# Layers 1 and 2 experts: two buffers for copied down weights, each copied in its slot's own step; 22 unread products instead of 40 ahead of layer 1's first rows

## What is computed

```python
def _L1_ffn_ref(x, Wr, W1, W2, W3):          # 8 experts, hidden width 352
    logits = tokens @ Wr
    probs = softmax(logits); topw, tope = top_k(probs, 2)
    gate = sum(one_hot(tope, E) * topw[..., None], axis=1)
    a = einsum('td,edh->teh', tokens, W2)
    b = einsum('td,edh->teh', tokens, W1)
    y = einsum('teh,ehd->ted', silu(a) * b, W3)
    out = einsum('ted,te->td', y, gate)
```

## Time and profile before

| | us |
|---|---|
| median of 3 runs | 817.55 |
| lowest and highest | 816.50 and 820.42 |
| the profiled execution, its own time | 818.61 |
| its span, first to last instruction | 816.8 |
| PE busy | 715.4 (88%) |
| DVE busy | 437.7 (54%) |
| POOL busy | 308.8 (38%) |
| ACT busy | 244.9 (30%) |
| mean granted TensorE clock, share of full speed | 0.937 |

### The profile page before, as it was taken

How to read it: one execution, slowest core, us unless ns; L and a number is a source line. 1 busy time by engine, 2 the same in 40 slices (tenths; PEclk the granted TensorE clock), 3 DMA queues, 4 the chain that set the end, 5 groups by cost and what they waited for, 6 DMA issues and landing times. The chain is left out here.

```text
span 816.8 us, 16930 instructions
## 1 busy us (share of the span) xinstructions
PE 715.4 (88%) x6115; PEld 577.2 (71%) x6115; DVE 437.7 (54%) x1155; ACT 244.9 (30%) x624; POOL 308.8 (38%) x365
## 2 busy tenths in 40 slices
PE   7997798899999889989896898798998878979997
PEld 5785687788888768844475686675433745879997
DVE  3766967545434365656534655675684367532212
ACT  1132411355445043124502411243364035111120
POOL 2346441456664140234214224411453187253211
PEclk9997997899999999899998799798998979899999
DMA  9403004788886439645324802100463244256603
GB/s 361 193 14 48 5 1 143 246 243 240 240 236 192 139 81 413 243 143 186 113 74 106 317 2 46 19 2 33 121 199 102 67 71 199 81 199 234 236 17 106
DMA packets 76553, 116.60 MB, mean 143 GB/s; under 512 B 44023, under 2 KB 57528, under 8 KB 73528
## 3 DMA queue, kind: packets, MB, share of 16 engines
q1 hardware_dynamic: 65141, 90.95, 35.3%
q0 software_dynamic: 6912, 17.31, 6.7%
q10 hardware_dynamic: 4418, 7.26, 2.4%
HBM read 100.34 MB, written 15.16 MB: 141 GB/s over the span
## 5 line engine op out<-in xcount | busy, mean ns | idle before, releaser
L280 PE MATMUL ps<-const_sb 128*128 128x128 f32 x946 | 126.4, 294 | 5.7 <-DMA const_sb<-in_consts 4.8
L280 PEld LDWEIGHTS ps<-const_sb 128*128 128x128 f32 x946 | 121.2, 208 | 9.0 <-DMA const_sb<-in_consts 4.8
L1878 PE MATMUL ps<-l0e_xg_fm,l0e_ring 128*128 128x128 f32 x544 | 72.7, 277 | 6.3 <-ACT l0e_up_sb L1968 2.5
L1878 PEld LDWEIGHTS ps<-l0e_xg_fm,l0e_ring 128*128 128x128 f32 x544 | 67.6, 191 | 12.2 <-issue 7.7
L955 PE MATMUL ps<-x_fm,w_sb 128*128 128x296 f32 x208 | 54.5, 414 | 4.6 <-PEq L237 4.3
L2473 PE MATMUL ps<-l_w,const_sb 128*32 x132 | 48.8, 506 | 7.7 <-DMA l1e_own_gu<-in_l_experts 3.0
L308 POOL TENSOR_TENSOR norm_r<-norm_ve,const_sb 128x2 f32<-128x2 f32 (+1 forms) x27 | 19.5, 724 | 92.5 <-DVE norm_ve L301 68.2
L955 PEld LDWEIGHTS ps<-x_fm,w_sb 128*128 128x128 f32 x208 | 39.1, 190 | 17.5 <-issue 6.1
L1784 POOL DMA_INDIRECT l0e_y_scratch<-l0e_y_tm,l0e_rows_u x34 | 35.6, 1047 | 32.3 <-ACT l0e_y_tm L1992 28.2
L413 ACT ACTIVATE x_fm<-ps 128x256 f32<-128x256 f32 x35 | 12.5, 383 | 107.5 <-PE ps L389 107.4
L1769 POOL DMA_INDIRECT l0e_xg_tm<-x_scratch,l0e_rows_u x34 | 33.3, 979 | 23.5 <-PE ps L1842 10.1
(11 more groups left out here) (518 smaller groups left out, 1635.0 us busy)
## 6 DMA issues: line engine op xcount, KB each, us to landing
l0e_ring<-in_l_experts SPq DMA_DIRECT2D x34, 514.0 KB
l_w<-in_l_experts SPq DMA_DIRECT2D x1, 8704.0 KB, 27.4
expert_w<-in_l_experts SPq DMA_DIRECT2D x4, 2048.0 KB
l_more_w<-in_l_experts SPq DMA_DIRECT2D x4, 2048.0 KB
l1e_own_gu<-in_l_experts SPq DMA_DIRECT2D x11, 704.0 KB
l_w<-in_l_experts SPq DMA_DIRECT2D x1, 6144.0 KB, 18.8
l2e_own_gu<-in_l_experts SPq DMA_DIRECT2D x11, 512.0 KB
l0e_down_w<-in_l_experts SPq DMA_DIRECT2D x1, 4096.0 KB
```

Of the source, the lines that this page charges most:

```text
L280: pe.matmul(ps[:, bank, 0:P], ident, ident, start=True, stop=True)
L1878: mm = pe.matmul(ps[0:widths[m], which, m * P:(m + 1) * P], w_n[:, c:c + widths[m]], x_n[:, k, :], start=(k == 0), stop=(k == KT - 1))
```

## The change

- `own_dn` gets two buffers; slot n uses n % 2.
- ACT and DVE copy the down weights of slot r in step r, where they copied those of slot r-1. The wait in front is the same one: in step r the down products of slot r-2 must be done, since that slot had the same buffer. For slots 0 and 1 there is no wait. DVE's loop has 11 steps instead of 12, and ACT's copies end a step earlier.
- In layer 1, 22 unread products stand ahead of `turn(0)` instead of 40.
- `ROWS` becomes an argument, whose default of 4 is what both calls use, so nothing follows from it.

```diff
-                own_dn = sb(f"{tag}_own_dn", [P, G - 1, MT * D], where=st)
+                own_dn = sb(f"{tag}_own_dn", [P, G - 1, 2, MT * D], where=st)
...
-                            stay_awake(pe, 40)
+                            stay_awake(pe, 22)
                             turn(0)
...
-                                                       own_dn[:, c - 1, m * D:(m + 1) * D] if c
+                                                       own_dn[:, c - 1, (e - S) % 2, m * D:(m + 1) * D] if c
...
-                            if 1 <= r <= NS:
-                                if r == 1:
+                            if 0 <= r < NS:
+                                if r == 0:
                                     act.wait_ge(s_expert, 1)
                                     act.wait_ge(s_all, all_ready)
                                 if r >= 2:
                                     act.wait_ge(s_down, S + r - 1)
                                 for c in mine["act"][1]:
-                                    theirs = held_by(act, r - 1, c)
-                                    act.activation(own_dn[:, c - 1, :], whole(theirs, GU, GU + MT * D), ACT.Copy)\
+                                    theirs = held_by(act, r, c)
+                                    act.activation(own_dn[:, c - 1, r % 2, :], whole(theirs, GU, GU + MT * D), ACT.Copy)\
                                         .then_inc(s_dn[c], 1)
...
-                                if n >= 1:
-                                    dve.wait_ge(s_down, S + n)
+                                if n >= 2:
+                                    dve.wait_ge(s_down, S + n - 1)
...
-                        for n in range(NS + 1):
-                            if n < NS:
-                                hidden(S + n)
-                                if n + 2 < NS:
-                                    copy_gu(n + 2)
-                            if n >= 1:
-                                copy_dn(n - 1)
+                        for n in range(NS):
+                            hidden(S + n)
+                            if n + 2 < NS:
+                                copy_gu(n + 2)
+                            copy_dn(n)
```

More of the change, by code:

```diff
@@ L2238, in column_experts @@
         def column_experts(tag, held, w_in, E, top, H, R, gu_by, dn_by, after, ahead=(), bias=None, dense=None, source=None,
-                           diag_in=None):
+                           diag_in=None, ROWS=4):
             G = P // R
@@ L2246, in column_experts @@
             NT = NS * G
-            ROWS, YS = 4, 3
+            YS = 3
             S, first = (0, 0) if dense is None else (TILES, 1)
@@ L2291, in column_experts @@
                 own_gu = sb(f"{tag}_own_gu", [P, G - 1, 2, GU], where=st)
-                own_dn = sb(f"{tag}_own_dn", [P, G - 1, MT * D], where=st)
-                xg_tm = row_sb[:, YS * D:(YS + ROWS) * D].rearrange("p (u d) -> p u d", d=D)
+                own_dn = sb(f"{tag}_own_dn", [P, G - 1, 2, MT * D], where=st)
+                xg_tm = row_sb[:, YS * D:(YS + ROWS) * D].rearrange("p (u d) -> p u d", d=D) if ROWS == 4 \
+                    else sb(f"{tag}_xg_tm", [P, ROWS, D], where=st)
                 xg_fm = const("pe")[:, 0:2 * KT * P].rearrange("p (u k r) -> p u k r", u=2, k=KT)
@@ L2713, in copy_dn @@
                             for c in mine["dve"][1]:
-                                if n >= 1:
-                                    dve.wait_ge(s_down, S + n)
+                                if n >= 2:
+                                    dve.wait_ge(s_down, S + n - 1)
                                 whose = experts[n, c] if (n, c) in experts else held_by(dve, n, c)
-                                dve.tensor_copy(own_dn[:, c - 1, :], whole(whose, GU, GU + MT * D)).then_inc(s_dn[c], 1)
+                                dve.tensor_copy(own_dn[:, c - 1, n % 2, :], whole(whose, GU, GU + MT * D))\
+                                    .then_inc(s_dn[c], 1)
                         dve.wait_ge(s_expert, 1)
```

## The result

| | before | changed |
|---|---|---|
| median, us | 817.02 (4 runs) | 805.07 (4 runs) |
| lowest to highest | 815.9 to 820.42 | 802.24 to 809.99 |
| the profiled execution's own time | 818.61 | 809.99 |
| its span | 816.8 | 808.2 |

The ratio is 0.9856, with a 95% interval of 0.9819 to 0.9893. Two later comparisons of the same two kernels gave 0.9872 (0.9822 to 0.9921) and 0.9887 (0.9853 to 0.9921). Ratios and intervals here leave out runs more than 1.5% above the fastest run of their kernel; the medians and ranges keep them. So the change saves 1.1 to 1.4% of the time, 9 to 12 us. The profiled execution happens to be the slowest of the four. Total times of this kernel scatter: on one chip 29 runs of the kernel before ranged from 806.6 to 823.1 us.

What follows compares the result with a forecast made beforehand. PE was taken as working nearly without a gap, idling for own_dn only at the loops' ends. Gains of 4.13 (front), 4.27 and 4.34 us (ends) sum to 12.7, off 818.61 gives 805.9 us; 8-in-10 range 802.5 to 810.0.

Steps and rivals of the forecast that it cites:

- The ends of the loops: Last two slots of each layer's loop: waits for own_dn and low clock vanish, 4.27 us in layer 1, 4.34 in layer 2.
- The landing: Behind each loop, the outputs' way back rather than unread products becomes the limit: 0.32 us saved in layer 1, 0.86 in layer 2.
- rival 1: Clock falls anyway at both ends, or mostly didn't fall before; only idle times go, 10.3 us, 808.3 us; chance 0.22.
- The front: Ahead of layer 1's slots: 18 unread products fewer at 0.2295 us each, gain 4.13 us.
- has landed at about 346.5, 0.8 us ahead of need: Layer 1's front: the first gather's rows are there before `turn(0)` at 347.32, so it needn't wait.
- A wait of `turn(0)` for the gather: Layer 1's front: listed first among signs of being wrong; `turn(0)` should follow the unread products without a wait.
- My bound of 3.3 us for the front: Layer 1's front: lowest gain allowed, for gather 0 landing 0.8 us late; upper bound 4.13.
- the second assumption: Layer 1's front: the unread products run at full clock, 0.2295 us each, 22 in 5.05 us.
- Rival 2: Layer 1's front: first rows late, two slots wait, 0.4 to 1.5 us lost, 807 us; chance 0.15 together with Rival 3.
- Rival 3: Loop ends: slot 10's hidden values late behind ACT's copy, 1.5 us lost, 807.4 us; chance 0.15 together with Rival 2.
- Rival 4: Layer 1's slots: fewer unread products drop the clock to 1.2 GHz, 809.4 us for one stretch, up to 833; chance 0.04.
- Rival 5: Loop ends: slot 10's copies still come last, so only the front's gain stays, 814.5 us; chance 0.02.

Runs made afterwards that it cites:

- Experiment 11: Changed kernel with 20 instead of 28 unread products behind the loops of layers 1 and 2: 807.89 us, ratio 0.9945 against the kernel before.
- experiment 2: Kernel before with only the front shortened, 22 instead of 40 unread products ahead of layer 1's slots, one buffer: 809.25 us, ratio 0.9965 against the kernel before.
- experiment 3: The changed kernel itself, run again on the first chip: 800.96 us, ratio 0.9872 against the kernel before.
- experiment 9: The changed kernel itself, run once more on the third chip: 804.68 us against 814.86 for the kernel before, ratio 0.9887.
- experiment 6: Changed kernel with 14 instead of 22 unread products ahead of layer 1's slots, second chip: 786.30 us, ratio 0.9843 against the kernel before.
- experiment 5: Changed kernel with none of the 22 unread products ahead of layer 1's slots: 791.06 us against 800.87 for the kernel before, ratio 0.9863.
- Experiment 7: Changed kernel, but in layer 1 ACT instead of DVE copies own_gu for slots 0 and 1: 787.68 us, ratio 0.9853 against the kernel before.
- experiment 4: Kernel before with unread products put into its four waits for own_dn: 811.37 us, ratio 0.9989 against the kernel before.
- experiment 1: Changed kernel with 40 unread products in front as before, so only the two buffers: 805.49 us against 814.17 for the kernel before, ratio 0.9916.
- experiment 8: Changed kernel with ACT making layer 1's own_gu copies for slots 0 and 1, and 14 unread products in front: 790.01 us, ratio 0.9882 against the kernel before.
- experiment 10: Changed kernel with 14 unread products ahead of layer 1's slots, third chip: 806.49 us, ratio 0.9902 against the kernel before.

## Why the prediction was right, and where a step was not

The time was right: 805.9 forecast, 805.07 measured, inside the range of 802.5 to 810.0, and faster as forecast. That the two differ by only 0.8 us is luck, since the forecast took 12.7 us off and the change is worth some 9 to 12.

**The ends of the loops** came out step by step. In layer 1 slot 9's down products followed the transposes without a wait, slot 10's waited 0.17 us for the hidden values (about 0.1 predicted), and the stretch shrank by 4.03 us (3.95). In layer 2 the wait was 0.48 us and the stretch shrank by 3.46 (3.48). Reading the page's 1.33 us "for line 2579" as a wait for `own_dn` was right: it is gone. The landing became what is late, as said, 0.22 us better than forecast in layer 1 and 0.31 worse in layer 2; PE idled 0.40 and 1.16 us for it, where I had said 0.6 to 0.9. Experiment 11 showed that it is the limit. The four waits of before, and the low clock that came with them, were the whole of the buffers' gain; the steady steps had none to give. (In the bounds of layer 2's end, 3.02 - 0.33 is 2.69 and not 2.6; rival 1 has it as 2.7, and nothing else uses it.)

**The front** was mis-sized. The term "18 x 0.2295 = 4.13 us" gave 2.80, 2.40, 2.39, 3.12 and 3.01 us from the sort to slot 0 in the five profiles with 22 products and DVE's copies (the changed kernel, experiments 2, 3, 9 and 11). The step that failed is the reading that gather 0 "has landed at about 346.5, 0.8 us ahead of need". `turn(0)` waited for it until 4.8 us after the gather's start in the first profile and 4.7 in experiment 11, where I had read 3.1. A wait of `turn(0)` for the gather was the first thing that I had named as a sign of being wrong, and it was there, 0.84 and 0.73 us.

The record of before already held this. I took 45 packets for a whole gather "with one or two at the cut". These are the counts of the gathers' queue in the kernel before, up to 3.2 us after the first gather's start (343.44 to 346.64 us) and from there to 4.7 us:

```profile
q0 software_dynamic: 45, 0.12, 12.1%
q0 software_dynamic: 51, 0.14, 32.7%
```

And the same in experiment 6, where the gather came early (331.34 to 334.54 us, and on to 336.04):

```profile
q0 software_dynamic: 48, 0.13, 14.5%
q0 software_dynamic: 48, 0.13, 28.7%
```

Both add up to 96 for two gathers, so a gather is 48 packets, and in the kernel before three of gather 0's can only have moved among gather 1's. "49 in the stretch of rows 3, which holds gather 1 alone" was wrong too. The changed kernel's first profile counts 45 and 51 as well, and experiment 11 counts 45 by 3.2 us. The profiles that count 47 or 48 by then show no late gather: `turn(0)` waited until 3.67 and 3.46 us in experiments 5 and 6, and in experiments 2, 3, 9 and 10 it didn't wait at all. Experiment 7 had 41 packets by 3.0 us, where its second gather's begin, and waited until 4.56. What holds the three packets back is not shown. One thing goes with it in all 13 profiles: in the five with the late packets (before, changed, 4, 7 and 11) a packet of 0.02 MB on an instruction queue (q8) began 2.2 to 3.0 us after the gather's start, in the other eight 1.6 us at most or not at all. My bound of 3.3 us for the front was too high to hold any of this.

In experiments 2 and 3 it was not the gather: there the second assumption failed, that the unread products run at full clock. In experiment 9 it was a late copy by ACT, whose cause is open. Rival 2 had named the late gather and its price, 0.4 to 1.5 us. The measured losses are 1.0 to 1.7, the two largest of them by the clock's fall behind the sort.

**What made up for it.** Two things that I hadn't worked out. The forecast took the whole sum off the profiled execution's 818.61 us, which lay 1.6 above the median of the four runs, and the first comparison was a favourable one: over three comparisons the gain was 11.8, 10.4 and 9.2 us. That is nearer to 10.3, what rival 1 gave, than to the 12.7 of the sum, and the two profiled executions differ by only 8.6 us (818.61 and 809.99). The front's shortfall of 1.0 to 1.7 us explains part of it. Whether the clock's share at the ends was also smaller on average is not settled: experiment 4 gave 0.9 us with an interval that holds 0 and 2.4, and against experiment 2's ends the changed kernel's are 7.5 us shorter instead of 8.6.

**The rivals.** Rival 1 had the clock fall at the ends all the same, or not fall in most executions of before. The first is out: it stayed 1.00 at the ends in every profile with two buffers and 28 products. For the second there are two profiles with the idle times, and both have the fall. Rival 3, a new wait for the hidden values, was 0.17 and 0.48 us, not 1.5 together. Rival 4's mechanism was real in experiments 5 and 6, with none and with 14 products. It cost 2.1 and 1.7 us, more than the earlier start gave, and never ran through the slots. With 22 products no profile shows it. Rival 5 is out. The waits for `own_gu`, which I kept as they were, came out 0.9 us shorter in layer 1 in the changed kernel's first profile (3.0 us before, 2.1), and this is the 0.94 in the table's fourth row. For slot 2 the wait was 1.38 to 2.60 us in the three profiles with 40 products and 1.19 to 1.61 in the five with 22. Whether the shorter front has a part in that or it only scatters is not settled.

**GpSimd beside DVE's copies.** The Trainium skill's "SBUF — State Buffer" ("Who interferes with whom") says that DVE's fp32 copies block GpSimd. Experiment 7 agrees in direction: gathers took 0.95 us instead of 1.30 without the copies. As the cause of the late first gather it doesn't stand: without the copies `turn(0)` still waited until 4.56 us after the gather's start, and with them it went ahead at 3.46 and 3.67 us in experiments 6 and 5, before they had ended (4.2 us). In the prediction I had set the rule aside because packets moved during the copies. That was right about the packets, and its 0.4 us off the front was on the right side, for another reason.

## What to carry to other kernels

A second buffer in a loop bound by another engine pays at the loop's ends, where the cover runs out. Read the last two steps in the timeline and not the loop's mean, and price what comes next (here the landing of the outputs). Unread products that hold TensorE's clock should last about as long as what they wait for. Shorter ones can give the start back in slower products behind it, as none did in front, 14 did in one profile of three, and 20 did behind. Before you take a gather for landed, count its packets against those of one that is known to be whole: three of 48 missing went with a start 1 us later. And before you put a lost microsecond down to an edit, look whether the clock had already fallen ahead of the first edited instruction.

## What the runs showed of the hardware

- A wait of 2.2 to 2.6 us of TensorE ahead of dense work was followed in four places (layer 1's end in the kernel before, experiments 1 and 11) by 1.2 GHz, 0.3 to 1.4 us into the work that came after. Waits of 0.4 to 1.3 us mostly were not, but 1.05 us ahead of the sort's last products was, in five profiles of 13 (experiments 2, 3, 5, 8 and 10), and so was 1.25 us ahead of the turning in experiment 6.
- In 29 and 24 runs of the kernel before, on two chips, the time at 1.2 GHz ranged over more than 30 us with nothing changed (79 to 116, and 82 to 113). A line through the runs of a chip gives 0.43 and 0.34 us of total time per us at 1.2 GHz, each within 0.1. That explains much of the scatter of 0.5% that hides terms of 2 us.
- The chips differ more than the change moves: the kernel before took 814.2, 814.9 and 800.9 us on three of them. Only comparisons on one chip mean anything here.
- Where TensorE waited for it, a first gather of 128 rows was there 3.5 to 4.8 us after GpSimd began to issue it, at the same place of the same program. Of the late ones, those of the changed kernel and of experiment 11 had three of their 48 packets outstanding at 3.2 us.
